# Turning every head pair's attention probabilities by DMA instead of on TensorE

## The reference

```
q = x @ wq.T + bq;  k = x @ wk.T + bk;  v = x @ wv.T + bv
q2 = (q @ wiq.T + biq).reshape(N, H, D).transpose(1, 0, 2)     # the same for k2, v2
scores = einsum('hnd,hmd->hnm', q2, k2) / 8 + mask[None]       # mask from 6144 edges
attn = softmax(scores, axis=-1)
out = einsum('hnm,hmd->hnd', attn, v2).transpose(1, 0, 2).reshape(N, OUT_F)
x = layernorm(x + out @ wo.T + bo)
```

## Time and profile before

| | us |
|---|---|
| median of 3 runs (lowest, highest) | 294.27 (293.76, 294.59) |
| the profiled execution's own time | 293.82 |
| its span | 292.1 |
| PE busy | 284.8 (98%) |
| DVE busy | 193.5 (66%) |
| ACT busy | 160.6 (55%) |
| POOL busy | 134.0 (46%) |

### The profile page before, as it was taken

How to read it: one execution, slowest core, us unless ns; L and a number is a source line. 1 busy time by engine, 2 the same in 40 slices (tenths; PEclk the granted TensorE clock), 3 DMA queues, 4 the chain that set the end, 5 groups by cost and what they waited for, 6 DMA issues and landing times.

```text
span 292.1 us, 5219 instructions
## 1 busy us (share of the span) xinstructions
PE 284.8 (98%) x1656; PEld 264.9 (91%) x1656; DVE 193.5 (66%) x486; ACT 160.6 (55%) x310; POOL 134.0 (46%) x114
## 2 busy tenths in 40 slices
PE   8999999999999999999999999999999999999991
PEld 8999999999999998888999999999999999787881
DVE  4889967566766674325157778787878687884085
ACT  5954423442344242421077777777777777697323
POOL 2000745645455542665855344545453535919400
PEclk9999999999999999999999999999999999999998
DMA  7959864463564439845120304030303121555013
GB/s 268 325 186 370 255 203 152 144 212 89 202 217 124 124 117 338 309 144 155 72 68 13 137 7 139 12 132 14 130 19 125 38 105 40 177 91 144 2 72 144
DMA packets 18766, 41.01 MB, mean 140 GB/s; under 512 B 7904, under 2 KB 8768, under 8 KB 18624
## 3 DMA queue, kind: packets, MB, share of 16 engines
q1 hardware_dynamic: 16640, 39.37, 40.9%
q0 software_dynamic: 1680, 0.62, 1.1%
q10 hardware_dynamic: 432, 0.85, 0.8%
HBM read 37.44 MB, written 2.21 MB: 136 GB/s over the span
## 4 chain that ended last, share of the span: by engine, by line
PE 91%; DVE 4%; POOL 1%; ACT 1%; issue 1%; POOLq 0%; DVEq 0%; ACTq 0%
PE bank L983 20%; PE bank L974 18%; PE bank L976 17%; PE bank L975 17%; PE bank L1090 5%; PE bank L1060 5%; PE bank L1072 4%; PE bank L999 3%; DVE stats L948 1%; PE bank L992 1%; POOL w_lo L351 1%; DVE res L947 1%; DVE shared L821 0%; ACT w_hi L433 0%; ACT shared L519 0%
## 5 line engine op out<-in xcount | busy, mean ns | idle before, releaser
L379 POOL DMA_INDIRECT mask_cells<-scratch x48 | 53.9, 1123 | 74.2 <-DMA mask_cells<-scratch 31.8
L351 POOL TENSOR_TENSOR w_lo<-w_raw,w_hi 128x1024 fp32r<-128x1024 f32 x18 | 42.9, 2403 | 47.7 <-DVE shared L832 43.0
L433 ACT ACTIVATE w_hi<-w_raw 128x1024 fp32r<-128x1024 f32 x49 | 51.3, 1053 | 19.4 <-PE bank L983 18.1
L974 PE MATMUL bank<-x_hi,w_hi 128*128 128x384 f32 x176 | 58.8, 334 | 0.0
L975 PE MATMUL bank<-x_lo,w_hi 128*128 128x384 f32 x176 | 58.8, 334 | 0.0
L976 PE MATMUL bank<-x_hi,w_lo 128*128 128x384 f32 x176 | 58.8, 334 | 0.0
L651 DVE TENSOR_TENSOR w_lo<-w_raw,w_hi 128x1024 fp32r<-128x1024 f32 x31 | 38.0, 1227 | 16.5 <-ACT w_hi L433 15.6
L974 PE MATMUL bank<-h_hi,w_hi 128*128 128x384 f32 x128 | 47.2, 369 | 0.0
L476 ACT ACTIVATE h_hi<-bank,bcol 128x384 f32 (+1 forms) x24 | 14.0, 582 | 55.1 <-PE bank L976 49.9
L976 PE MATMUL bank<-h_hi,w_lo 128*128 128x384 f32 x128 | 43.1, 337 | 0.0
L975 PE MATMUL bank<-h_lo,w_hi 128*128 128x384 f32 x128 | 42.9, 335 | 0.0
(11 more groups left out here) (107 smaller groups left out, 522.1 us busy)
## 6 DMA issues: line engine op xcount, KB each, us to landing
w_raw<-weights SPq DMA_DIRECT2D x53, 512.0 KB
shared<-key_rows SPq DMA_DIRECT2D x6, 512.0 KB
shared<-start SPq DMA_DIRECT2D x5, 320.0 KB, 5.9
res<-x_rows SPq DMA_DIRECT2D x1, 1536.0 KB, 6.9
out<-res SPq DMA_DIRECT2D x6, 256.0 KB, 2.0
mask_cells<-scratch POOLq DMA_INDIRECT x48
shared<-start ACTq DMA_DIRECT2D x2, 320.0 KB, 5.2
mask_cells<-mask SPq DMA_DIRECT2D x1, 576.0 KB, 6.1
```

The source lines that it names most:

```text
L351: nc.gpsimd.tensor_tensor(lo, w_raw[:, s, cols], hi.bitcast(F32), ALU.subtract)\
L379: nc.gpsimd.indirect_dma_start(out=mask_cells, out_offset=bass.IndirectOffsetOnAxis(ap=cell[:, c:c + 1], axis=0), in_=cell_value[:, c:c + ...
L433: nc.scalar.activation(w_part(t, s, slice(0, F))[0], w_raw[:, s, :], ACT.Copy).then_inc(w_hi_done, 1)
L974: pe.matmul(out_ps, w_hi[:, s, cols], moving_hi, start=(k == 0), stop=False)
```

## The change

All eight pairs now go the way of the last one, and the TensorE transposes are gone. In a step the scores are those of pair `j - 1`, as before, while the casts of the turned planes and the value products are those of pair `j - 2`. The high planes are written by POOL (`high_planes`, a `tensor_scalar` from float32 to fp16), the low planes by DVE from the float32 tile and the high plane (a `scalar_tensor_tensor` whose two tensor inputs are both in SBUF), into the first half of the float32 tiles they come from. `invert` multiplies the sums by a tile of constants, `downs`, where it took a constant before. POOL no longer waits for `probs_ready` ahead of the weight tiles, and its order in a step is: weight tile, six high planes, values' low part, weight tile, `att_low`. SP issues four transposing DMAs a pair between the weight loads, and the last pair's four all ahead of the last weight load. The rings of turned tiles have four places. The projection's order of blocks is other, too. The core of the diff:

```diff
-TRANSPOSES_FROM, VALUES_FROM = 2, 5
+VALUES_FROM = 1
+
+PT_RING = 4
...
-        plane_lo = [v2[:, h, 0:NT * N // 2].bitcast(FP16).rearrange("p (b n) -> p b n", b=NT) for h in range(2)]
+        plane_lo = [probs_flat[:, NT * N * h:NT * N * h + NT * N // 2].bitcast(FP16).rearrange("p (b n) -> p b n", b=NT)
+                    for h in range(2)]
...
-            def turn(h):
...
+            def turn(a, h):
+
+                sp.wait_ge(plane_hi_done, 2 * NT * a + NT * (h + 1))
+                if a:
+                    sp.wait_ge(pt_hi_done, 2 * NT * (a - 1) + NT * (h + 1))
                 sp.dma_start_transpose(turned_hi[:, h, :, :, :].rearrange("p b m q -> p (b m) q"),
                                        plane_hi[:, h, :, :].rearrange("p b n -> p (b n)"))\
                   .then_inc(turned_hi_landed[h], 16)
-                sp.wait_ge(plane_lo_done, NT * (h + 1))
+                sp.wait_ge(plane_lo_done, 2 * NT * a + NT * (h + 1))
+                if a:
+                    sp.wait_ge(pt_lo_done, 2 * NT * (a - 1) + NT * (h + 1))
                 sp.dma_start_transpose(turned_lo[:, h, :, :, :].rearrange("p b m q -> p (b m) q"),
                                        plane_lo[h].rearrange("p b n -> p (b n)"))\
                   .then_inc(turned_lo_landed[h], 16)
 
             for t in range(2 * RING, TILES):
...
                 if t == TILES - 1:
-                    turn(0)
+                    for h in range(2):
+                        turn(PAIRS - 1, h)
                 load_tile(t, t % RING)
...
+                a, odd = divmod(t - PAIR_TILE - 2 * RING, 2)
+                if 0 <= a < PAIRS - 1 and not odd:
+                    for h in range(2):
+                        turn(a, h)
...
+            def high_planes(a):
+                for place in range(2 * NT):
+                    h, b = divmod(place, NT)
+                    if b == 0:
+                        pool.wait_ge(inv_ready, 2 * a + (h + 1))
+                        if not (isinstance(a, int) and a == 0):
+
+                            pool.wait_ge(turned_hi_landed[h], 16 * a)
+                        nc.gpsimd.sem_inc(inv_seen, 1)
+                    nc.gpsimd.tensor_scalar(plane_hi[:, h, b, :], probs[:, place, :], row_inv[:, place:place + 1],
+                                            None, ALU.mult).then_inc(plane_hi_done, 1)
...
-                if not (isinstance(j, int) and j == 0):
-                    v_low(j - 1, 1 - par)
-
-                    pool.wait_ge(probs_ready, 2 * NT * j)
                 low_part(t + LEAD, s0)
...
+                    high_planes(j - 1)
+                    v_low(j - 1, 1 - par)
...
             low_part(WO_TILE + 2, 2)
+            high_planes(PAIRS - 1)
             low_part(WO_TILE + 3, 3)
...
+                if more:
+                    turned_high(j - 2, par, range(0, NT))
                 split(t + LEAD, s0, raws)
...
+                    turned_high(j - 2, par, range(NT, 2 * NT))
                 evacuate(t, L1_TILES + 2 * j, par, 0)
-                if attend:
-                    pt_high(a, (2, 3))
-                if not (isinstance(j, int) and j < 2):
-                    att_high(a - 1)
-                if attend:
-                    pt_high(a, (4, 5))
+                if more:
+                    att_half_out(j - 2, 0)
+                split(t + LEAD + 1, s0 + 1, raws)
+                if more:
+                    att_half_out(j - 2, 1)
                 evacuate(t + 1, L1_TILES + 1 + 2 * j, par, 1)
-                if attend:
-                    att_half_out(a, 0)
-                else:
-                    split(t + LEAD + 1, s0 + 1, raws)
+                if more:
+                    att_high(j - 2)
...
+            turned_high(a - 1, 0, range(0, NT))
+            v_high(a, 1)
+            exps(a)
+            turned_high(a - 1, 0, range(NT, 2 * NT))
             split(WO_TILE + 3, 3, (WO_TILE + 3) // RING + 1)
...
+                if place % NT == 0 and not (isinstance(a, int) and a == 0):
+
+                    dve.wait_ge(turned_lo_landed[place // NT], 16 * a)
...
+            def invert(a, h):
+
+                dve.wait_ge(exp_done, 2 * NT * a + NT * (h + 1))
+                cols = slice(NT * h, NT * (h + 1))
+                then_settle(nc.vector.tensor_tensor(row_inv[:, cols], row_sum[:, cols], downs[:, :], ALU.mult))
                 then_settle(nc.vector.reciprocal(row_inv[:, cols], row_inv[:, cols]))
-                dve.sem_inc(inv_ready, len(places))
-
-            def low_planes(places):
+                dve.sem_inc(inv_ready, 1)
...
+            def low_planes(a, places):
                 for place in places:
-                    i = ROW_TILES[place]
-
-                    dve.wait_ge(plane_hi_done, place + 1)
-                    nc.vector.scalar_tensor_tensor(out=plane_lo[i % 2][:, i // 2, :], in0=probs[:, i, :], scalar=row_inv[:, i:i + 1],
-                                                   in1=plane_hi[:, i % 2, i // 2, :], op0=ALU.mult, op1=ALU.subtract)\
-                        .then_inc(plane_lo_done, 1)
-
-            def turned_low(groups):
+                    h, b = divmod(place, NT)
+
+                    if b:
+
+                        dve.wait_ge(plane_lo_done, 2 * NT * a + place)
+                    dve.wait_ge(plane_hi_done, 2 * NT * a + (place + 1))
+                    nc.vector.scalar_tensor_tensor(out=plane_lo[h][:, b, :], in0=probs[:, place, :],
+                                                   scalar=row_inv[:, place:place + 1], in1=plane_hi[:, h, b, :],
+                                                   op0=ALU.mult, op1=ALU.subtract).then_inc(plane_lo_done, 1)
...
-                for place in range(4):
+                if before is not None:
+                    turned_low(before, par, range(0, NT))
+                for place in range(5):
                     mask_scores(a, place)
-                normalise(a, (0, 1))
-                mask_scores(a, 4)
-                normalise(a, (2,))
+                invert(a, 0)
                 mask_scores(a, 5)
-                normalise(a, (3, 4))
-                pt_low(a, (0,))
-                normalise(a, (5,))
-                pt_low(a, (1,))
-                pt_low(a, (2,))
-                if u is not None:
-                    evacuate_pair(u, par, 0)
-                pt_low(a, (3,))
+                if before is not None:
+                    turned_low(before, par, (NT,))
+                low_planes(a, (0,))
+                invert(a, 1)
+                low_planes(a, (1,))
+                if before is not None:
+                    turned_low(before, par, (NT + 1,))
+                low_planes(a, (2,))
+                if before is not None:
+                    turned_low(before, par, (NT + 2,))
+                low_planes(a, (NT,))
+                if q_tile is not None:
+                    evacuate_pair(q_tile, par, 0)
+                low_planes(a, (NT + 1,))
+                if before is not None:
+                    add_halves(before, 0)
+                low_planes(a, (NT + 2,))
+                if before is not None:
+                    add_halves(before, 1)
...
-                    pe.wait_ge(probs_ready, 2 * NT * a + NT * (h + 1))
...
-                for b in range(NT):
-                    ins = pe.transpose(pt_bank(g)[:, b * P:(b + 1) * P],
-                                       probs[:, 2 * b + h, m * P:(m + 1) * P], ident[:, :])
-                ins.then_inc(pt_ready, 1)
...
+                    if not (isinstance(a, int) and a == PAIRS - 1):
+
+                        pe.wait_ge(masked, 2 * NT * a + 3 * NT)
+
+                pe.wait_ge(pt_hi_done, 2 * NT * a + (g + 1))
                 pe.wait_ge(pt_lo_done, 2 * NT * a + (g + 1))
...
-                            if k >= VALUES_FROM:
-                                values(a, 1 - par, k - VALUES_FROM)
-                            if 0 <= k - TRANSPOSES_FROM < 2 * NT:
-                                transposes(a, k - TRANSPOSES_FROM)
+                        if which == 1 and more and 0 <= k - VALUES_FROM < 2 * NT:
+                            values(j - 2, par, k - VALUES_FROM)
...
+            project(0, 2)
+
 
             pe.wait_ge(masked, 2 * NT * a + 4)
-            project(1, 0, right)
-            project(1, 1, right)
-            for k in range(2, 4):
-                project(0, k)
+            for k in range(3):
                 project(1, k)
-
-            pe.wait_ge(masked, 2 * NT * a + 2)
+            for g in range(2 * NT):
+                values(a - 1, 0, g)
+            project(0, 3)
+            project(1, 3)
...
-            for k in range(6, KT):
-                last = project(0, k)
-            for ins in last:
+            for ins in project(0, KT - 1):
                 ins.then_inc(y_ready, 1)
-            for k in range(6, KT):
-                last = project(1, k)
-            for ins in last:
+            for ins in project(1, KT - 1):
                 ins.then_inc(y_ready, 1)
```

234 lines of the change are left out of this document (76 added, 158 removed).

## The result

The changed kernel takes 311.54 us (308.87 to 314.51, four runs) against 294.1 for the kernel before (293.76 to 294.59); the ratio is 1.056 [1.048, 1.065]. The forecast was 298.0, its range ended at 305.5. With two more runs, 311.35 and 313.18, its times lie in two groups, 308.9 to 309.3 and 311.4 to 314.5; the ratio compares the mean of the four lowest of the six, 310.7, with 294.1, and by the lower group alone it would be 1.051. The profile shown here is of an execution at 313.78 (span 312.0).

The account below looks back on a forecast made before the run. PE was taken as the bound, busy 284.8 of 292.1 us. -14.2 + 8.5 + 3.0 + 2.5 + 3.0 + 1.4 = +4.2 on 293.82 gave 298.0; the range ran from 287.6 to 305.5.

Parts of the forecast that it names:

- the high plane was under-priced: Sign for the whole kernel: what a median over 303 us would mean about POOL's high plane.
- What goes from PE: TensorE: 42 groups of transposes and their roundings go, 14.2 us; a step on PE falls from 14.5 to 12.4.
- The other streams: Loop step of 12.4: DVE 12.1, POOL 11.5 with high planes at 0.75 each, ACT 11.2; each alone would fit.
- Where DVE and POOL meet: Loop: a two-input DVE instruction and a POOL instruction reading SBUF exclude each other; the second waits, 0.95 and 0.59 seen.
- the step that follows: Loop: with DVE and POOL exclusive a step takes 14.1, bounds 12.4 to 15.3; five periods cost +8.5 us.
- Entering the loop: Steps 1 to 2: POOL's weight tiles hold DVE's first inversion, planes and evacuation follow late; 3.0 us, 1.3 without exclusion.
- (1): Tail: second projection block waits for POOL's weight tile behind six planes and the values' low part; 2.5 us.
- (2): Tail: fourth block's weights are rounded on ACT behind pair 6's last casts, then handled by POOL; +3.0 us.
- (3): Tail: the release of DVE's norm chain comes later against PE's whole work, and the end with it; 1.4 us.
- (4): Transposing DMAs land in 3.2 to 5.1 us; costed at nothing, up to 0.6 a step in one of 12.4.
- The dearer rival: Loop: high plane on POOL as dear as a two-input operation (1.02), full exclusion; step 15.3, 306.5 us; chance 0.13.
- No exclusion, 288.6: Loop: rival that DVE's low planes run beside POOL unhindered and the gain comes through; 288.6 us, chance 0.30.

Follow-up runs that it names:

- micro_ops: Not the layer: seven short sections timing single POOL and DVE operations with the layer's shapes, alone and side by side; POOL's scaling took 1.23 us alone.
- plane_half: The changed kernel with each high plane on POOL over only half its columns; 297.87 us, ratio 1.013.
- entry_wait: The changed kernel with POOL waiting, in step 1 alone, for DVE's sixth low plane before the values' low part and two weight tiles; 309.15 us, 1.051.
- plane_cast: The changed kernel with the scaling of the high planes left out, POOL only casting each tile; 310.0 us, a period of 16.3.
- four_two: The changed kernel with two of six high planes on ACT and the fourth projection tile ahead of the last pair's planes; 308.7 us, 1.048.
- tail_order: The changed kernel with the fourth projection tile ahead of the last pair's planes; 306.6 us, 1.043.
- plane_cast_wait: High planes only cast on POOL, unscaled, plus a wait each step: POOL begins the second weight tile after DVE's six low planes; 300.3 us, 1.020.
- planes_act: The changed kernel with the three high planes of each pair's second head on ACT instead of POOL; median 312.3 us.
- micro_holds: Not the layer: six short sections with POOL's two-input instructions beside other forms of DVE operations; strided casts took 0.47 us each, not held.

## Why the prediction was wrong

The direction and most of the waits it named were right, though not that high planes would be held in the loop (they stayed at 1.24). What failed is the price of POOL's high plane, and with it the length of a step. The prediction's own sign for a median over 303, "the high plane was under-priced", says the same. By its own steps:

**What goes from PE** (-14.2): nearly right. In the period from 197.49 to 212.69 four gaps between PE's starts, of 0.44 to 1.38, make 2.5 more than the usual spacing; without them the step is 12.7, where I had 12.4.

**The other streams.** This is the step that failed. "From below 0.51, from above 1.02, I take 0.75": measured 1.25. The upper bound was no bound. It assumed that one input less cannot cost more, and micro_ops shows the reverse for POOL (0.96 for two tensors, 1.23 for one and a scalar). With the same words and 1.25 put in, POOL's stream would have been 7.0 + 7.5 = 14.5 beside the measured 14.6, and the bound of the loop plain. plane_half has a plane near the price that the forecast took and comes to 297.87, which gives back 11.3 us against entry_wait. That it meets the forecast's 298.0 is partly luck: by the table's intervals it is 2.0 shorter than forecast from S1 to S2 (11.33), 2.3 shorter from S2 to S7 (68.24), 2.5 longer from S7 to T (17.15) and 1.7 longer from T to the end (50.72).

**Where DVE and POOL meet, and the step that follows** (14.1, +8.5): 15.2, so +14 over the step of 12.4; 5.6 of the miss of 11.4 at the lower level. Exclusion exists, but I applied it to the wrong partner. POOL's scalings do not exclude a low plane, they stretch it by 0.1 to 0.3; its two-input instructions do, for their whole length. The forecast's own sum for full exclusion, with 1.25 put in, would have been 14.5 + 3.5 - 1.6 = 16.4, too long by 1.2. In the steady step what was held is the inversion's product, by 0.5. And in plane_cast and four_two, with less time in planes on POOL, low planes did meet the weight tiles: the dear planes were also what kept them clear of these. The rule cited from the Trainium skill ("SBUF — State Buffer", Who interferes with whom) is borne out by the two-input pairs, 2.2 to 2.8 in place of 0.6, and not by the scalings, where neither engine waited for the other's whole instruction.

**Entering the loop** (3.0): PE's wait ahead of step 2 is 2.46. Behind it the upper level has 3.85 more, for a low plane that was held for five instructions of POOL in a row; the forecast let DVE in between any two. Without that plane S1 to S2 is 13.66 (entry_wait) against the 13.3 of the forecast.

**The tail.** (1) 2.5 forecast, 3.88 measured, and with cheaper planes, in plane_half, its longest wait for POOL is still 3.6. What the sum forgot is that the other engines' pace, counted for five periods, rules this interval too (17.9 against 14.6): the longer wait makes 1.4 of these 3.3, a wait of 1.05 for DVE's cast another part. (2) 3.0 forecast (4.6 less four value groups of 0.35 is 3.2), 2.32 and 0.40 measured; tail_order gives 2.5 for it. (3) The norm chain takes 14.5 from its release to the end in both kernels (277.55 to 292.1, and 293.04 to 307.6 in entry_wait), so its release moves the end, as said; the 1.4 by itself was not tested. (4) The landing cost a steady step nothing but 0.3 before a mask.

**The rivals.** The dearer rival had the right mechanism at its first half (a plane as dear as or dearer than the two-input one) and came nearest with 306.5. Its second half, full exclusion, did not happen; that its step of 15.3 meets the measured 15.2 is luck, since it put the plane at 1.02, too low, and the holding too high. Its 0.13 was too little and the range, ending at 305.5, cut it off. "No exclusion, 288.6" would have needed what plane_cast_wait has, planes of 0.58 and no meeting: 300.3. So 288.6 was far too low even for its own case. I put that down to summing DVE's instructions and not the chain through four engines, which is argued and not shown.

Left open: why a low plane is once held for a single instruction of POOL and once for five, by what it is decided when the low plane starts 0.13 behind in both cases, and what the 13.8 to 15.1 of a step consist of once POOL's planes are cheap.

## What to carry to other kernels

Price an operation on an engine by a row of the same form, and where there is none, widen the upper end past the nearest "bigger" form: on POOL a tensor times a scalar cost 1.23 and a tensor times a tensor 0.96. Before work is moved to POOL, ask which of DVE's two-input instructions will now meet POOL's two-input ones; relieving POOL made the period of this kernel 1 us longer three times (plane_cast, planes_act, four_two) and shorter once (plane_half), and a single wait that keeps the two apart gave 1.6 to 2.0 us a step back. When the bottleneck engine gets a shorter stream, follow the chain through all engines for one period, not only the sums of each.

## What the runs showed of the hardware

POOL, 128x384 from float32: scaling 1.23 (in the layer 0.75 for 192 columns where it met nothing, so by an estimate from the two some 0.3 of it does not depend on the width), cast 0.48, two-input product 0.96 (micro_ops, plane_half). DVE held behind a POOL weight tile of 1.9 to 2.5: low plane 2.25, contiguous fp16 cast 2.10 for 0.35, contiguous scaling 2.50 for 0.42, each as single records (micro_ops, micro_holds). Not held: strided casts to fp32r and one input in PSUM (micro_holds). Beside POOL's scalings low planes of 0.60 and 0.93 took turns (micro_ops). DMA transposes of 128x1152 in 2 bytes landed 3.2 to 5.0 us after issue, 3.3 at the median, four a step beside the weight loads, and delayed in a steady step nothing but one mask, by 0.3 (the changed kernel).
